# A gated-delta attention and FFN kernel: k's and v's token rows stored half by half, and every engine's work per turn in a new order

## What is computed

```python
qkvz = (hidden_states @ w_qkvz.T).reshape(Bsz, Sl, NH, 2 * DK + 2 * DV)
mixed = lax.conv_general_dilated(mixed, conv_w, (1,), [(K_CONV - 1, 0)], ...)   # 4 taps over time, on q, k, v
q = _l2norm(q) * DK ** (-0.5)
k = _l2norm(k)
def step(Sstate, xs):
    q_t, k_t, v_t, g_t, b_t = xs
    Sstate = Sstate * jnp.exp(g_t)[..., None, None]
    kv = jnp.einsum('bhk,bhkv->bhv', k_t, Sstate)
    delta = (v_t - kv) * b_t[..., None]
    Sstate = Sstate + k_t[..., :, None] * delta[..., None, :]
    o_t = jnp.einsum('bhk,bhkv->bhv', q_t, Sstate)
    return (Sstate, o_t)
o = o * lax.rsqrt(var + EPS) * norm_weight * jax.nn.sigmoid(z)
return o.reshape(Bsz, Sl, VDIM) @ w_out.T
...
x = x + _layernorm(_L0_attn_ref(_layernorm(x, axis=-1), ...), axis=-1)
x = x + _layernorm(_L0_ffn_ref(_layernorm(x, axis=-1), ...), axis=-1)
```

## Time and profile before

| what | value |
|---|---|
| time, median of 3 runs | 3099.59 us (3080.13 to 3100.36) |
| time of the profiled execution | 3095.35 us |
| its span, first to last instruction | 3093.5 us |
| PE busy | 2889.1 us (93%) |
| DVE busy | 2445.7 us (79%) |
| ACT busy | 1752.3 us (57%) |
| POOL busy | 1103.3 us (36%) |
| mean granted clock of TensorE | 0.980 |

### The profile page before, as it was taken

How to read it: one execution, slowest core, us unless ns; L and a number is a source line. 1 busy time by engine, 2 the same in 40 slices (tenths; PEclk the granted TensorE clock), 3 DMA queues, 4 the chain that set the end, 5 groups by cost and what they waited for, 6 DMA issues and landing times. The chain is left out here.

```text
span 3093.5 us, 101425 instructions
## 1 busy us (share of the span) xinstructions
PE 2889.1 (93%) x42816; PEld 1953.0 (63%) x42816; DVE 2445.7 (79%) x5610; ACT 1752.3 (57%) x3242; POOL 1103.3 (36%) x904
## 2 busy tenths in 40 slices
PE   6699999999999999999999999999999999789998
PEld 3366666666666666666666666666666666655555
DVE  7688888888888888888888888888888888656554
ACT  6456666566556666666566566656666566424332
POOL 1444344444444444343444444444343344100000
PEclk9899999999999999999999999999999999899999
DMA  5454545554545555554455555544455445300000
GB/s 154 79 82 84 89 80 83 83 98 81 81 81 97 80 81 84 93 83 80 81 98 84 82 80 99 83 76 83 75 100 81 80 81 84 83 21 21 27 14 21
DMA packets 1298099, 241.85 MB, mean 78 GB/s; under 512 B 1248240, under 2 KB 1269104, under 8 KB 1296496
## 3 DMA queue, kind: packets, MB, share of 16 engines
q1 hardware_dynamic: 1297648, 235.36, 44.2%
HBM read 120.13 MB, written 39.58 MB: 52 GB/s over the span
## 5 line engine op out<-in xcount | busy, mean ns | idle before, releaser
L1342 PE MATMUL bank<-xT,w_sb 128*128 128x512 f32 x2048 | 982.1, 613 | 10.0 <-PEq L516 5.2
L784 POOL TENSOR_TENSOR kq<-kq,product 128x510 f32<-128x510 f32 (+2 forms) x384 | 448.9, 1182 | 723.4 <-ACT kq L873 713.4
L1342 PEld LDWEIGHTS bank<-xT,w_sb 128*128 128x128 f32 x2048 | 372.3, 191 | 374.4 <-issue 346.1
L772 POOL TENSOR_TENSOR dec_ap<-gcrow,gcb 128x1024 f32<-128x1024 f32 x64 | 121.8, 1902 | 657.2 <-DMA gcb<-gcb_d 657.2
L1088 DVE SCALAR_TENSOR_TENSOR kq<-bank,cw,kq 128x510 f32<-128x510 f32 (+2 forms) x384 | 285.7, 744 | 58.8 <-ACT kq L873 49.5
L1088 DVE SCALAR_TENSOR_TENSOR v_c<-bank,cw,v_c 128x510 f32<-128x510 f32 (+2 forms) x384 | 285.8, 744 | 15.9 <-ACT v_c L873 6.9
L1353 PE MATMUL bank<-kq 64*64 64x128 f32 x4096 | 276.7, 273 | 20.4 <-POOL kq L784 8.3
L940 ACT COPY delta<-bank 128x256 f32<-128x256 f32 x256 | 95.2, 372 | 341.8 <-PE bank L1410 341.5
L1457 PE MATMUL bank<-wo,u_sq 128*128 128x256 f32 x1024 | 261.0, 399 | 4.0 <-DVE u_sq L1180 3.5
L879 ACT ACTIVATE product<-bank,cw 128x512 f32<-128x512 f32 x384 | 249.1, 684 | 6.8 <-PE bank L1342 2.8
L1435 PE MATMUL bank<-ap_mat,delta 64*64 64x64 f32 x4096 | 243.0, 219 | 3.2 <-issue 3.1
(11 more groups left out here) (168 smaller groups left out, 5459.4 us busy)
## 6 DMA issues: line engine op xcount, KB each, us to landing
xT<-xT_d SPq DMA_DIRECT2D x64, 512.0 KB, 3.9
gcrow<-gcrow_d SPq DMA_DIRECT2D x128, 256.0 KB, 4.6
k_r<-k_tok SPq DMA_DIRECT2D x512, 64.0 KB, 2.3
v_r<-k_tok SPq DMA_DIRECT2D x512, 64.0 KB
a_d<-ap_mat SPq DMA_DIRECT2D x256, 64.0 KB
z_t<-z_d SPq DMA_DIRECT2D x256, 64.0 KB, 2.5
w_sb<-in_w_qkvz SPq DMA_DIRECT2D x8, 1024.0 KB, 6.8
x_un<-eye_un SPq DMA_DIRECT2D x64, 128.0 KB, 4.0
```

The costliest lines, as they stand in the source:

```text
L784: nc.gpsimd.tensor_tensor(t[:, :, d:SEQ], t[:, :, d:SEQ], prod[:, :, 0:SEQ - d], ALU.add).then_inc(tap_added[i], 1)
L1342: ins = nc.tensor.matmul(bank[:, :], w_two[m.grp % 2][:, h, s * P:(s + 1) * P], xT[:, h, :], start=(h == 0), stop=(h == HT - 1))
```

## The change

There are two parts.

**The layout of the token rows.** `k_tok`, `k_r` and `v_r` keep their size, but hold the first 32 numbers of all 16 chunk columns, then the second 32. A helper views a tile in that way:

```diff
+            def by_half(t):
+                return t[:, :, :].rearrange("p g c -> p (g c)").rearrange("p (f g c) -> p f g c", f=2, c=W2)
+            def over_halves(t):
+                return t.rearrange("p (o g x) -> p o g x", o=1, x=1).broadcast_to([P, 2, G, W2])
...
-                                    sp.dma_start(dst[r:r + W2, :, W2 * f:W2 * f + W2], k_tok[q:q + W2, :, W2 * t:W2 * t + W2]) \
+                                    sp.dma_start(by_half(dst)[r:r + W2, f, :, :], by_half(k_tok)[q:q + W2, t, :, :]) \
...
-                        ins = nc.vector.transpose(k_tok[:, a * GP:(a + 1) * GP, :].rearrange("p g c -> p (g c)"), v_c[:, a, :])
+                        ins = nc.vector.transpose(by_half(k_tok)[:, :, a * GP:(a + 1) * GP, :], v_c[:, a, :].rearrange("p (g f c) -> p f g c", f=2, c=W2))
...
-                        nc.vector.tensor_tensor(kt[m.par][:, :, :], k_r[:, :, :], col(e_tail).broadcast_to([P, G, C]), ALU.mult).then_inc(kt_done, 1)
+                        nc.vector.tensor_tensor(kt[m.par][:, :, :].rearrange("p g (f c) -> p f g c", f=2), by_half(k_r), over_halves(e_tail), ALU.mult).then_inc(kt_done, 1)
...
-                                                       rhs[half, i, :] if c else v_r[m.par][half, g, :], start=True, stop=True)
+                                                       rhs[half, i, :] if c else by_half(v_r[m.par])[half, :, g, :], start=True, stop=True)
```

**The order.** `DEPTH` goes from 6 to 5 and the calls of all five `turn` functions stand in a new order, with the waits that this needs (`eend_done` is new, others go to another index). The places of the banks in `ring` change with it. Of each `turn` one line shows the kind of edit:

```diff
-        DEPTH = 6
+        DEPTH = 5
...
+                        if s[0]:
+                            wait_for(pe, x_T_in, s[0], 16)
+                            wait_for(pe, mats_done[3], s[0], 1, back=1)
+                            project(s[0], 0, ring(s[0], 0))
```

More of the change, by code:

```diff
@@ L1560, in turn @@
-                        if s[3]:
-                            wait_for(pe, zoff_done, s[3], 1)
-                            solve(s[3], 0)
+                        if s[3]:
+                            wait_for(pe, delta_done[0], s[3], 1)
+                            advance(s[3], 0)
+                        if s[1]:
+                            wait_for(pe, conv_done[1], s[1], 1)
+                            project(s[1], 3, ring(s[1], 2))
+                        if s[3]:
+                            wait_for(pe, og_done[0], s[3], 1, back=1)
+                            output(s[3], 0)
+                            wait_for(pe, state_done[0], s[3], 1)
+                            key_state(s[3], 1)
@@ new lines, in turn @@
+                        if s[4]:
+                            wait_for(pe, tap_prod[2], s[4], 1, back=-3)
+                            wait_for(pe, og_done[0], s[4], 1)
+                            project_out(s[4], 0, ring(s[4], 3))
+                        if s[3]:
+                            wait_for(pe, rhs_done[1], s[3], 1)
+                            solve(s[3], 1)
+                        if s[1]:
+                            wait_for(pe, z_exp[1], s[1], 1)
+                            project(s[1], 5, ring(s[1], 0))
@@ new lines, in turn @@
+                        if s[3]:
+                            wait_for(pe, delta_done[1], s[3], 1)
+                            advance(s[3], 1)
+                            output(s[3], 1)
+                            wait_for(pe, state_done[1], s[3], 1)
+                            key_state(s[3], 2)
+                        if s[4]:
+                            project_out(s[4], 1, ring(s[4], 1))
+                        if s[3]:
+                            wait_for(pe, rhs_done[2], s[3], 1)
+                            solve(s[3], 2)
@@ new lines, in turn @@
+                        if s[1]:
+                            wait_for(pe, acc_done[0], s[1], 1, back=3)
+                            project(s[1], 4, ring(s[1], 1))
+                        if s[3]:
+                            wait_for(pe, delta_done[2], s[3], 1)
+                            advance(s[3], 2)
+                            output(s[3], 2)
+                            wait_for(pe, state_done[2], s[3], 1)
+                            key_state(s[3], 3)
+                        if s[1]:
+                            wait_for(pe, tap_added[2], s[1], 1)
+                            scores(s[1], 1, ring(s[1], 3))
+                            wait_for(pe, tap_added[5], s[1], 1)
+                            scores(s[1], 3, ring(s[1], 2))
```

610 lines of the change are left out of this document (280 added, 330 removed).

## The result

The changed kernel takes 3123.69 us (median of 4 runs, 3121.1 to 3124.5) where before takes 3093.38 us beside it (4 runs, 3080.13 to 3100.36): ratio 1.0101, 95% interval 1.0065 to 1.0137. It is 30 us slower; 3020 us was forecast, 2958 to 3092 at most. What moved is seen in the same views as before.

The account below looks back on a forecast made before the run. PE, busy 93% of the span, was taken as the bound. State -30, z_t -10, instruction gaps -29, clock -19 and new waits +12 sum to -76 us from 3095.35, so 3020 us, range 2958 to 3092.

Parts of the forecast that it names:

- The floor: PE's clean turn of 38.04 us, 2320.4 us for 61 turns, taken as the floor for the same matmuls.
- the clean turn itself is longer: Sign that the forecast is wrong: PE's best turn above 37.9 to 38.1 us because a form got dearer.
- New waits: PE's solve(m, 0) on ACT's outer_out and scores on DVE's conv 4: 0.1 us per turn each, +12 us.
- with that v_r lands 4 us earlier: SP's eight issues of v_r fall from 7.79 to 4 us, more gain than turn_k's longest wait of 1.6 us.
- State wait: Key_state of chunk 1 on PE waits for DVE's copy of the state: 32.2 to 2 us, -30 us.
- z_t: Join16_inner's wait on PE for z_t, back from DRAM, goes: -10 us.
- Instruction gaps: PE running out of instructions in long stretches of small matmuls: 41.9 us become 20, other rows 27.3 become 20, -29 us.
- Clock: PE's excess busy time of 39.2 us follows the gaps and is halved with them: -19 us.
- Layout at 0: The changed layout forms on DVE, ACT and PE cost the same as before: 0 us.
- The slower one: Rival: PE starves from project(m, 4) to join16_outer, with gaps, clock and new waits growing: 3160 us, chance 0.12.
- The waits only move: Rival: DVE's conv 4 or ACT's outer_out replaces state and z waits at 0.7 us per turn: 3090 us, chance 0.12.

Follow-up runs that it names:

- e1_layout: The kernel before with the new layout alone, all orders and DEPTH as before: 3058.38 us, ratio 0.9972 to before.
- f1_k_late: The changed kernel with both turn_k calls moved on DVE from ahead of new_state(0) to behind residual(1): 3076.95 us, ratio 1.0014 to before.
- E7_p0_apart: The kernel before with project(m, 0) moved on PE from behind join16_outer to ahead of it: 3157.97 us, ratio 1.0268 to before.

## Why the forecast was wrong

**The floor.** "Nothing but fewer or cheaper ones goes below it, and the change has as many": the step is true as far as it goes and was used as if nothing could go above it. The same matmuls in another sequence took 0.97 us more per turn, +59 us where the forecast had 0. This is the first step that failed. The rows to see it by were there: the earlier trace rows has three projections in a row at 5.42 us, 1.81 each, and the clean turn of before has 1.92 for one between two small groups. I had named "the clean turn itself is longer" as what would prove me wrong, but with a dearer form as its cause, and that fell with e1_layout.

**New waits.** This is the second step that failed. +12 us for solve(m, 0) on outer_out and scores on conv 4. Neither has a row. The wait that came is solve(m, 1) on residual(1), 80.1 us, +68 over the term. It hangs on the step above it, "with that v_r lands 4 us earlier": counted from the end of turn_v its issues are done 2.7 us later. The layout took 0.4 to 0.5 us off the eight issues, as the pieces hardly set them, and the rest of their fall to a median of 5.7 us, still not 4, goes with the order, which put x_un into the dear place ahead of them. And I counted SP's queue ahead of z_out but not ahead of v_r, where the wait on e_end (85 us in the run) and x_un now stand. How much the wait on e_end does by itself no run tested. I had myself written that new_state(0) stands behind turn_k in DVE's order, before and after; residual(1) does too. That this place makes the wait, f1_k_late shows.

**State wait.** 32.2 to 2 forecast, 5.7 measured: right in size, and by the projection between advance and key_state, since v_r came later and not earlier.

**z_t.** -10 forecast, the row is gone: right.

**Instruction gaps.** 69 us to 40 forecast, 21 measured: right in sign, and 19 us too careful. The instruction packets are 341 as before. The Trainium skill, page "Runtime: NRT & Kernel Launch", section "Instruction fetch mechanics", has a crossing mostly hidden, by which the gaps would have another cause and stay. The gaps went where the forecast's count of small matmuls in a row said: join16_outer, now behind a projection, has 3.4 us for 32.2, and join16_inner the largest row, 13.1. E7_p0_apart, with one projection set ahead of join16_outer, has no issue row there either, but its PE also stands there for the matrices (58.7 us), so it does not tell a long group from a pause. What the gap is made of inside PE's supply no run here shows.

**Clock.** Busy time above clean turns 39.2 to 20 forecast, 16.4 measured: right; the mean granted clock of the 61 turns went from 0.99 to 1.00.

**Layout at 0.** Right on PE (37.89 us with it). Its gain on v_r's issues and landing, some 0.8 us per turn, shows in the time by 0.3% in the old order, which noise could make, and by 15 us (1.1% by the ratios) in the new one.

**The rivals.** The slower one, PE starving between project(m, 4) and join16_outer, did not happen: that stretch has fewer gaps. "The waits only move" was nearest in kind, with other waits in view and 43 us for what became 80. No rival had a longer clean turn, so none could have reached the measured time by the right cause. The sum with the measured terms: -26.5 - 10.5 - 47.6 - 22.8 + 80.1 + 59.2 = +31.9 us.

## What to carry to other kernels

When a new order keeps all instructions of the busiest engine, lay out its turn by start-to-start times and price each kind of neighbour, as a group costs more or less by what stands next to it; a best turn is the floor of its order only. When one transfer is issued from an in-order queue, count what is moved ahead of it there, and on the receiving engine count everything that stands behind the instruction that waits for it, needed or not. Try a moved instruction by itself: here one transpose set behind new_state(0) and one left ahead of it as filler won 0.4%, and both moved lost 0.8% against the kernel with the layout alone.

## What was not expected of the hardware

- A projection of four 128x512 matmuls takes 1.81 us from start to start beside another long group and 1.91 to 1.92 between two groups of 64-wide matmuls; 16 matmuls of 64x64 take 0.51 us with a small group behind them and 0.61 with a long one. Cutting a pair of such neighbours in two cost 0.33 us, and in the other pair 0.48 with a stop in it.
- The time of SP's issues followed the pieces little and the place in the queue much. Eight issues of 64 KB (v_r, medians): 8.4 us with pieces of 128 B and 7.9 with 2 KB in the old order, 6.1 and 5.7 in the new one, and 8.1 with 2 KB when x_un, ahead of them, is taken away. X_un's own issue is 0.53 us elsewhere and 2.96 there. The packets fell from 1297648 to 806128 (page's queue rows) and the landing by 0.3 us only.
